# Shared-expert outputs through DRAM as a fifth combine term, three pick buffers and a shorter routing chain in a macaron mixture-of-experts kernel

## The chip, the cores and the metric

One core of one Trainium2 chip runs the whole kernel. The core has five engines that run their own instruction streams and wait for one another by semaphores: TensorE (PE in the profile, its weight loads PEld), VectorE (DVE), ScalarE (ACT), GpSimd (POOL) and SyncE (SP), which here only starts DMAs. The metric is device time in microseconds, the median of several executions; the profile is of one execution.

## The reference

The input x has 4 x 512 tokens of 256 channels, so 2048 tokens. The block is a "macaron": half a feed-forward layer, a scan layer, and the same half feed-forward layer again.

```python
x = L0_attn_x
x = x + 0.5 * _L0_ffn_ref(_layernorm(x), ...)     # gate, shared, 16 routed experts
x = x + _L0_attn_ref(_layernorm(x), ...)          # y_t = a_t * y_(t-1) + x_t, between projections
x = x + 0.5 * _L0_ffn_ref(_layernorm(x), ...)
# in _L0_ffn_ref:
scores = sigmoid(logits) + gate_b
weights, indices = top_k(scores, 4); weights /= weights.sum(-1)
shared_out = (silu(x @ w1_shared) * (x @ w3_shared)) @ w2_shared      # hidden size 176
h3 = silu((x @ w1_routed[e]) * (x @ w3_routed[e]))                    # for the 4 chosen experts e
routed_out = sum over the 4 of weight * (h3 @ w2_routed[e])
return shared_out + routed_out
```

## The kernel before, in words

The tokens lie in 16 tiles of 128 (`NT = 16`). The residual stream stays in SBUF as `xres`. A feed-forward pass `f` (0 or 1) has these stages.

*Norm stage*, 16 tiles. GpSimd normalises a tile (`norm`) into a ring of four buffers, SyncE writes it to `xn_dram` (`xn_out`), TensorE transposes it (`turn_x`), ScalarE copies the high part (`xs_high`), VectorE makes the low part (`xs_low`), and TensorE multiplies by the shared weights and the gate (`hidden`). Products that need float32 accuracy are done as three products of high and low parts (`mm3`). In pass 0 SyncE also loads the routed experts two at a time between the `xn_out`s (`load_experts`, after tiles 1, 4, 7, 10, 13 and 15). Each loaded expert needs a high copy (`high_up`, `high_down`, on ScalarE) and low parts (`low_up` on VectorE for the experts in `DVE_UP`, `low` on GpSimd for the rest). Experts 12 to 15 share their SBUF with the scan layer, so they are loaded and split again in pass 1.

*Routing, shared and pick stage.* VectorE finds the top four of 16 (`route_members`), TensorE counts the members with matmuls (`count`: `p_pre`, L1038, and `p_tot`, L1040), VectorE works out slots (`route_slots`). Meanwhile the shared expert is finished in steps: `shared_step(n)` is, on TensorE, the transpose of hidden tile n (`turn_hidden`, L1012) and the output product of tile n-1 (`shared_out`, L1025), which ends with a matmul by twice the identity that adds `xres` (L1027); on ScalarE, the copy of the transposed tile (`copy_hidden`, L469) and the eviction of tile n-2 with scale 0.5 to `xres` (`evict`, L474). Steps 2 to 9 (`SH_ENDS = 10`) come before the picks, the other seven between them (`picked`). A pick `t` turns the slots of 128 tokens into rows of a token list: VectorE compares (`pick`, L769 and L771), ScalarE scales (`scale_pick`, L487), TensorE multiplies (L1052). The tiles of a pick have two buffers, so that VectorE and ScalarE wait for `s_pkd` of pick t-2. In pass 0 ScalarE's in-order program has one `high_expert` before each of the shared steps 2 to 9, and five more among the picks, expert 15 last; in pass 1 it has experts 12 to 14 ahead of steps 5 to 7 and 15 after pick 13.

*Routed stage*, `NS = 80` slots of 128 rows. GpSimd gathers token rows by indirect DMA (`gather`), four buffers deep; TensorE transposes, multiplies with the slot's expert, transposes the hidden tile, multiplies again; ScalarE and VectorE sit between; SyncE writes the result to `ys_dram` (`y_out`). TensorE enters only after waits for `s_yo` (all shared tiles evicted), `s_rt` (routing ready) and `s_wla`, `s_wlo` (all weight splits done), and the gather of slot 0. On GpSimd the program order is: gathers 0 to 3, then `low_expert(15)`, then gather 4 and the rest.

*Combine.* GpSimd gathers, for each token tile, the rows of the four chosen slots (`combine`, L370, four buffers `cg`); VectorE adds them with their weights to `xres` (L790), two tiles interleaved. In pass 0 the scan layer (L1096 to L1127 on TensorE) runs behind it in chunks of two tiles, in pass 1 SyncE writes the output.

## Time and profile before

| what | value |
|---|---|
| median of 3 runs | 727.38 us (724.78 to 810.8) |
| the profiled execution's own time | 726.9 us |
| its span, first to last instruction | 725.1 us |
| mean granted TensorE clock | 0.868 |
| PE, PEld, DVE, ACT, POOL busy | 73%, 67%, 61%, 47%, 48% of the span |

The span of the profiled execution is 1.8 us shorter than its time. The stages lie, roughly, at: norm stage 7 to 38 us, routing, shared steps and picks 38 to 83, routed stage 92 to 265, combine and scan layer 270 to 384, and then the second pass with its norm stage to 407, routing to 448, routed stage 457 to 631, combine to the end. An engine's busy share is a mean over stages with different limits, so each stage is read by itself.

### The profile page before, as it was taken

The page shows a single profiled execution, that of the slowest core. Times are in us where ns is not written, and L with a number is a line of the kernel's source. Part 1 is how long each engine was busy: PE and PEld are TensorE (multiplying, and loading weights), DVE is VectorE, ACT ScalarE, POOL GpSimd, SP SyncE. Part 2 cuts the span into 40 slices and gives each one's busy share as a digit, 9 for nine tenths or more (in the row PEclk, how much of TensorE's full clock was granted, in tenths as well). Part 3 has the DMA queues.
Part 4 walks back from the last instruction along what each step waited for, and adds up shares of the span by engine and source line. Part 5 has one row for each costly group of instructions (what it writes and reads, how often), then busy time and mean ns, then how long its engine had stood idle before and what let it go on. Part 6 is the DMA issues. An engine that isn't in the chain of part 4 may idle for free.

```text
span 725.1 us, 14307 instructions
## 1 busy us (share of the span) xinstructions
PE 528.3 (73%) x3442; PEld 488.8 (67%) x3443; DVE 440.1 (61%) x1253; ACT 341.3 (47%) x1001; POOL 344.6 (48%) x355
## 2 busy tenths in 40 slices
PE   4887489999999970586667896799999999800000
PEld 3765389999999970365547674699999999700000
DVE  5486547777777753567844686377777777513233
ACT  3568445555555540365564465355555555400000
POOL 2379544444444407777404022544444444067774
PEclk9989879999999995788898989799999999955555
DMA  8950224443434423333202300234343435234443
GB/s 263 298 166 31 66 79 123 126 123 123 123 123 123 122 73 101 102 101 98 64 0 99 108 31 10 81 123 125 121 125 120 128 121 121 80 99 125 130 132 99
DMA packets 51577, 79.92 MB, mean 110 GB/s; under 512 B 8485, under 2 KB 37541, under 8 KB 51549
## 3 DMA queue, kind: packets, MB, share of 16 engines
q0 software_dynamic: 13824, 37.77, 19.3%
q1 hardware_dynamic: 37725, 41.82, 17.6%
q8 instruction: 13, 0.21, 0.1%
q14 instruction: 15, 0.12, 0.1%
HBM read 52.29 MB, written 27.26 MB: 110 GB/s over the span
## 4 chain that ended last, share of the span: by engine, by line
PE 55%; POOL 20%; issue 12%; DMA 4%; ACT 4%; DVE 3%; SPq 0%; POOLq 0%; DVEq 0%; ACTq 0%
PE bank L925 40%; POOL mamba_room L370 17%; PE bank L947 5%; PE bank L981 5%; DMA xn_scratch<-ring_f 3%; POOL ring_f L360 2%; PE bank L1025 2%; ACT ring_f L487 2%; DMA ys_scratch<-ring_f 1%; PE bank L1012 1%; ACT w_routed L406 1%; PE bank L1027 1%; PE bank L990 1%; ACT xres L474 1%; PE bank L1052 1%
## 5 line engine op out<-in xcount | busy, mean ns | idle before, releaser
L925 PE MATMUL bank<-w_routed,ring_r 128*128 (+1 forms) x1920 | 314.7, 313 | 2.8 <-DVE ring_r L647 1.6
L925 PEld LDWEIGHTS bank<-w_routed,ring_r 128*128 128x128 f32 (+1 forms) x1920 | 282.7, 191 | 4.6 <-issue 4.5
L360 POOL DMA_INDIRECT ring_f<-xn_scratch,tokidx x160 | 155.4, 972 | 207.7 <-PE bank L947 176.8
L370 POOL DMA_INDIRECT mamba_room<-ys_scratch,si x128 | 126.6, 989 | 74.5 <-issue 38.4
L790 DVE SCALAR_TENSOR_TENSOR xres<-mamba_room,wk,xres 128x256 f32<-128x256 f32 (+1 forms) x128 | 53.4, 478 | 97.2 <-DMA mamba_room<-ys_scratch,si 97.2
L663 DVE TENSOR_TENSOR ring_f<-bank,ring_f 128x176 f32<-128x176 f32 x160 | 54.5, 341 | 57.7 <-ACT ring_f L441 57.6
L441 ACT ACTIVATE ring_f<-bank 128x176 f32<-128x176 f32 x160 | 50.8, 317 | 81.5 <-PE bank L925 81.5
L655 DVE TENSOR_TENSOR ring_r<-bank,ring_r 88x256 fp32r<-88x256 f32 x160 | 67.3, 421 | 33.3 <-ACT ring_r L433 28.7
L447 ACT ACTIVATE ring_f<-ring_f 128x176 f32<-128x176 f32 x160 | 56.1, 351 | 65.4 <-DVE ring_f L663 65.4
L647 DVE TENSOR_TENSOR ring_r<-bank,ring_r 128x256 fp32r<-128x256 f32 x160 | 66.0, 413 | 17.1 <-ACT ring_r L425 17.1
L673 DVE COPY ring_f<-bank 128x256 f32<-128x256 f32 x160 | 67.8, 424 | 13.2 <-DMA ys_scratch<-ring_f 2.3
L947 PE MATMUL bank<-cst,ring_f 128*128 128x128 f32 x320 | 62.3, 279 | 16.5 <-POOL w_routed L334 16.5
L425 ACT ACTIVATE ring_r<-bank 128x256 fp32r<-128x256 f32 x160 | 59.6, 373 | 17.1 <-PE bank L947 17.1
L981 PE MATMUL bank<-cst,ring_f 128*88 128x128 f32 x320 | 61.5, 273 | 0.0
L433 ACT ACTIVATE ring_r<-bank 88x256 fp32r<-88x256 f32 x160 | 58.0, 362 | 1.1 <-PE bank L981 1.1
L334 POOL TENSOR_TENSOR w_routed<-raw_routed,w_routed 88x512 fp32r<-88x512 f32 (+1 forms) x31 | 44.3, 1456 | 28.9 <-ACT w_routed L409 28.8
L1104 PE MATMUL bank<-mamba_room,stage 128*128 128x256 f32 x128 | 41.4, 480 | 22.4 <-ACT mamba_room L578 21.1
L947 PEld LDWEIGHTS bank<-cst,ring_f 128*128 128x128 f32 x320 | 40.7, 143 | 17.5 <-issue 17.2
L1104 PEld LDWEIGHTS bank<-mamba_room,stage 128*128 128x128 f32 x128 | 30.0, 242 | 31.7 <-ACT mamba_room L578 24.6
L353 POOL TENSOR_SCALAR ring_f<-xres,rstd,nmr 128x256 f32<-128x256 f32 x32 | 18.1, 575 | 61.7 <-DVE nmr L640 41.9
L925 PE MATMUL bank<-w_shared,ring_r 128*128 128x368 f32 x192 | 43.5, 373 | 0.1
L981 PEld LDWEIGHTS bank<-cst,ring_f 128*88 128x88 f32 x320 | 37.1, 123 | 0.2
(118 smaller groups left out, 562.6 us busy)
## 6 DMA issues: line engine op xcount, KB each, us to landing
ys_scratch<-ring_f SPq DMA_DIRECT2D x160, 128.0 KB, 1.7
raw_routed<-in_w13r SPq DMA_DIRECT2D x6, 704.0 KB
xn_scratch<-ring_f SPq DMA_DIRECT2D x32, 128.0 KB, 2.3
raw_routed<-in_w13r SPq DMA_DIRECT2D x8, 352.0 KB
ring_f<-xn_scratch,tokidx POOLq DMA_INDIRECT x160
raw_routed<-in_w2r SPq DMA_DIRECT2D x6, 352.0 KB
xres<-in_x_in SPq DMA_DIRECT2D x4, 512.0 KB, 5.9
mamba_room<-ys_scratch,si POOLq DMA_INDIRECT x128, 2.8
```

Of the source, the lines that this page charges most:

```text
L360: pool.indirect_dma_start(xg[j % UN], None, xn_dram, bass.IndirectOffsetOnAxis(ap=tokidx[:, j:j + 1], axis=0)).then_inc(s_g[j % UN], 16)
L370: pool.indirect_dma_start(cg[t % 4][:, q, :], None, ys_dram, bass.IndirectOffsetOnAxis(ap=si[:, n:n + 1], axis=0)).then_inc(s_cg[t % 4], 16)
L425: act.activation(xT[b][0], p_xT[b][:, 0:DC * P], ACT.Copy).then_inc(s_xhi, 1)
L433: act.activation(hT[b][0][0:HC, :], p_hT[b][0:HC, 0:2 * P], ACT.Copy).then_inc(s_hhi, 1)
L447: act.activation(hid[c % 2], hid[c % 2], ACT.Silu).then_inc(s_s, 1)
L647: dve.tensor_tensor(xT[b][1], p_xT[b][:, 0:DC * P], xT[b][0].bitcast(f32), ALU.subtract).then_inc(s_xlo, 1)
L655: dve.tensor_tensor(hT[b][1][0:HC, :], p_hT[b][0:HC, 0:2 * P], hT[b][0][0:HC, :].bitcast(f32), ALU.subtract).then_inc(s_hlo, 1)
L673: dve.tensor_copy(yb[b], p_y[b][:, 0:D]).then_inc(s_yo, 1)
L925: last = pe.matmul(out, a, b, start=(q == 0), stop=(q == len(terms) - 1))
L947: last = pe.transpose(p_xT[b][:, q * P:(q + 1) * P], xg[k][:, q * P:(q + 1) * P], ident)
L981: last = pe.transpose(p_hT[b][0:HC, q * P:(q + 1) * P], hid[b][:, q * HC:(q + 1) * HC], ident)
L1104: last = pe.matmul(out[:, e * MCH:(e + 1) * MCH], m_w[m][:, q * D + e * P:q * D + (e + 1) * P], src[:, q * MCH:(q + 1) * MCH], start=(q == ...
```

## The change

- `shared_out` on TensorE loses the matmul by `twice`; its eviction goes to one of two new buffers `sh_out` in `ring_f`, and waits for `s_sw` of tile t-2. SyncE writes each to `sh_dram` (16 DMAs of 128 KB per pass) and, after the last `y_out`, reads them back into a fifth place of the combine's buffers (`TERMS = 5`). VectorE adds it by a plain `tensor_tensor`. The next use of a buffer waits for the fifth term.
- Pick tiles have three buffers; VectorE and ScalarE wait for pick t-3.
- VectorE makes the high copies of experts 0 to 3 in pass 0's norm stage (t = 7 to 10) and their low parts at t = 11 to 14. ScalarE's copies there are experts 4 to 6; 7 to 14 lie ahead of shared steps 2 to 6 (two, two, two, one, one), and only expert 15 is left among the picks, after pick 11.
- `DVE_UP` is 0, 1, 2, 3, 15, so GpSimd takes the upper low parts of 13 and 14. `low_expert(15)` comes before the gathers, and before GpSimd's wait for `s_rt`.
- `route_slots`: one product over all four choices in place of four, and no casts back to float; the pick compares with int32 operands. `count` reads `oh` as it lies and writes `p_tot` with a stride.
- SyncE: `twice` isn't loaded; the final output loop is unrolled, with the fifth term's loads in it.

```diff
-DVE_UP = (0, 1, 2, 13, 14, 15)
+NHD = 4
+DVE_UP = (0, 1, 2, 3, 15)
+CHAIN_HIGHS = {2: (7, 8), 3: (9, 10), 4: (11, 12), 5: (13,), 6: (14,)}
+TERMS = TOPK + 1
...
+        sh_out = [ring_f[:, 1536 + b * D:1536 + (b + 1) * D] for b in range(2)]
...
+            def shared_out(f, t):
+                sp.wait_ge(s_yo, f * STEPS + t + 1)
+                sp.dma_start(sh_dram[t * P:(t + 1) * P, :], sh_out[t % 2]).then_inc(s_sw[t % 2], 16)
+
+            def shared_in(f, t):
+                if t >= 4:
+                    sp.wait_ge(s_cd, term(f, t - 4, TERMS - 1))
+                sp.dma_start(cg[t % 4][:, TOPK, :], sh_dram[t * P:(t + 1) * P, :]).then_inc(s_cs[t % 4], 16)
...
                 for e in range(MAMBA_E, NE - 1):
                     load_late(e)
+                for t in range(6):
+                    shared_out(f, t)
                 sp.wait_ge(s_ht, f * STEPS + 8)
                 load_late(NE - 1)
+                for t in range(6, NT):
+                    shared_out(f, t)
...
-                for e in range(0 if f == 0 else MAMBA_E, NE - 1):
-                    low_expert(e, e + 1 + f * (NE - MAMBA_E))
+                for e in range(0 if f == 0 else MAMBA_E, NE):
+                    low_expert(f, e)
                 pool.wait_ge(s_rt, f + 1)
                 for k in range(UN):
                     pool.wait_ge(s_xw[k], 16 * (NT // UN) * (f + 1))
-                for j in range(UN):
-                    gather(f, j)
-                low_expert(NE - 1, NE + f * (NE - MAMBA_E))
-                for j in range(UN, NS):
+                for j in range(NS):
                     gather(f, j)
...
             def evict(f, t):
                 act.wait_ge(s_y, f * STEPS + t + 1)
-                act.activation(xres[:, t, :], p_yS[t % 2][:, 0:D], ACT.Copy, scale=0.5).then_inc(s_yo, 1)
+                if t >= 2:
+                    act.wait_ge(s_sw[t % 2], 16 * (f * (NT // 2) + t // 2))
+                act.activation(sh_out[t % 2], p_yS[t % 2][:, 0:D], ACT.Copy, scale=0.5).then_inc(s_yo, 1)
...
                 for n in range(2, SH_ENDS):
                     if f == 0:
-                        high_expert(f, n + 1)
+                        for e in CHAIN_HIGHS.get(n, ()):
+                            high_expert(f, e)
...
-                    if f == 0 and t % 3 == 1 and t < 12:
-                        high_expert(f, SH_ENDS + 1 + t // 3)
-                    if t == 13:
+                    if t == 11:
                         high_expert(f, NE - 1)
...
-                for k in range(TOPK):
-                    last = dve.tensor_tensor(prod[:, :, k, :], oh[:, :, k, :], sl, ALU.mult)
-                link(last)
+                link(dve.tensor_tensor(prod, oh, sl.unsqueeze(2).broadcast_to((P, NT, TOPK, NE)), ALU.mult))
...
-                dve.tensor_copy(lof, p_loi)
-                link(dve.tensor_copy(hif, p_hii))
...
-                for q in range(TOPK):
+                for q in range(TERMS):
...
+                        if q == TOPK:
+                            dve.wait_ge(s_cs[2 * c + b], 16 * (f * (NT // 4) + i + 1))
...
+                            dve.tensor_tensor(xr, xr, cg[2 * c + b][:, q, :], ALU.add).then_inc(s_cd, 1)
...
-                    if f == 0 and t in (12, 14):
-                        low_up(t // 2 - 6, t // 2 - 5)
+                    if f == 0 and 7 <= t < 7 + NHD:
+                        high_expert(t - 7)
+                    if f == 0 and 7 + NHD <= t < 7 + 2 * NHD:
+                        low_up(f, t - 7 - NHD)
...
+                for b in range(2):
+                    dve.wait_ge(s_sw[b], 16 * (NT // 2) * (f + 1))
                 pipeline(dve, NS, [(LAG_X, dve_x(base)), (LAG_H, dve_product(base)),
...
-                pe.matmul(p_yS[t % 2][:, 0:D], twice, xres[:, t, :], start=False, stop=True).then_inc(s_y, 1)
...
-                    last = pe.matmul(p_tot, hcst[:, H_ONE:H_ONE + P], oh[:, :, k, :].rearrange("p t e -> p e t"),
+                    last = pe.matmul(p_tot.rearrange("p (e t) -> p t e", e=NE), hcst[:, H_ONE:H_ONE + P], oh[:, :, k, :],
```

## Rows read from the trace of the kernel before

**Rows 1.** The page's chain that ended last, by line, in shares of the span.

```profile
PE bank L925 40%; POOL mamba_room L370 17%; PE bank L947 5%; PE bank L981 5%; DMA xn_scratch<-ring_f 3%; POOL ring_f L360 2%; PE bank L1025 2%; ACT ring_f L487 2%; DMA ys_scratch<-ring_f 1%; PE bank L1012 1%; ACT w_routed L406 1%; PE bank L1027 1%; PE bank L990 1%; ACT xres L474 1%; PE bank L1052 1%
```

**Rows 2.** Busy time by stretch, then granted TensorE clock, DMA share and GB/s.

```profile
45.00:50.00 5.00, 5.00 (x17) 3.06 (x15) 3.01 (x10) 2.25 (x5) 3.44 (x3) 0.54 0.43 131
...
430.00:440.00 10.00, 7.79 (x65) 5.86 (x66) 9.30 (x19) 6.04 (x15) 0.00 (x0) 1.00 0.00 0
```

**Rows 3.** The chain in order of time, end of pass 0's picks: start, length.

```profile
79.82 0.68 ACT w_routed L406
...
81.02 0.91 ACT ring_f L487 x2
...
82.71 0.16 DVE tokidx L778
...
83.14 3.13 POOL ring_f L360
```

**Rows 4.** The same chain at the end of pass 1's picks.

```profile
446.09 0.91 ACT ring_f L487 x2
...
448.20 3.00 POOL ring_f L360
```

**Rows 5.** ScalarE's timeline: start, length, what.

```profile
26.26 0.80 ACT L406 ACTIVATE w_routed<-raw_routed 128x704 fp32r<-128x704 f32 x1
...
60.42 1.04 ACT L487 ACTIVATE ring_f<-ring_f,cst 128x320 f16<-128x320 f16 x2
...
428.91 1.00 ACT L487 ACTIVATE ring_f<-ring_f,cst 128x320 f16<-128x320 f16 x2
```

**Rows 6.** TensorE's timeline, its idle time and who ended it in brackets.

```profile
45.19 1.88 PE L1040 MATMUL bank<-ring_f,hcst 128*128 128x256 f16 x4
...
52.77 1.03 PE L1025 MATMUL bank<-raw_shared 88*128 88x256 f32 x4
53.64 0.60 PE L1027 MATMUL bank<-xres,stage 128*128 128x256 f32 x2
...
92.14 1.09 PE L947 MATMUL bank<-cst,ring_f 128*128 128x128 f32 x4 [8.40 <-POOL w_routed L334]
...
456.89 1.09 PE L947 MATMUL bank<-cst,ring_f 128*128 128x128 f32 x4 [8.07 <-POOL w_routed L334]
```

**Rows 7.** VectorE's timeline in pass 0.

```profile
26.14 0.42 DVE L678 TENSOR_TENSOR ring_r<-bank,ring_r 128x256 fp32r<-128x256 f32 x1 [3.78 <-ACT ring_r L454]
...
31.68 0.88 DVE L689 TENSOR_TENSOR w_routed<-raw_routed,w_routed 128x704 fp32r<-128x704 f32 x1
...
51.79 1.42 DVE L755 TENSOR_TENSOR ring_f<-ring_f,bank 128x256 f32<-128x256 f16 x4
...
55.30 0.23 DVE L762 CAST bank<-bank 128x64 f32<-128x64 int32 x1
...
55.70 0.49 DVE L769 TENSOR_TENSOR ring_f<-hcst,bank 128x320 f16<-128x320 f16 x1
56.10 0.68 DVE L771 TENSOR_TENSOR ring_f<-hcst,bank 128x512 f16<-128x512 f16 x1
...
61.50 0.49 DVE L769 TENSOR_TENSOR ring_f<-hcst,bank 128x320 f16<-128x320 f16 x1 [3.72 <-PE bank L1052]
```

**Rows 8.** GpSimd's timeline in pass 0.

```profile
29.03 1.63 POOL L353 TENSOR_SCALAR ring_f<-xres,rstd,nmr 128x256 f32<-128x256 f32 x3 [3.02 <-DMA xn_scratch<-ring_f]
...
34.24 5.05 POOL L334 TENSOR_TENSOR w_routed<-raw_routed,w_routed 88x512 fp32r<-88x512 f32 x3
...
49.46 24.32 POOL L334 TENSOR_TENSOR w_routed<-raw_routed,w_routed 88x512 fp32r<-88x512 f32 x17 [1.08 <-ACT w_routed L409]
```

**Rows 9.** DMA issues of the page: KB each, median us from issue to landing.

```profile
ys_scratch<-ring_f SPq DMA_DIRECT2D x160, 128.0 KB, 1.7
...
mamba_room<-ys_scratch,si POOLq DMA_INDIRECT x128, 2.8
```

**Rows 10.** VectorE's last combine, at the end of pass 1.

```profile
719.71 2.86 DVE L790 SCALAR_TENSOR_TENSOR xres<-mamba_room,wk,xres 128x256 f32 x7 [4.12 <-DMA mamba_room<-ys_scratch,si]
```

More of the change, by code:

```diff
@@ L180, in build @@
         s_wsd = sem("shared_down_loaded")
+        s_cs = [sem(f"shared_fetched{b}") for b in range(4)]
+        s_sw = [sem(f"shared_written{b}") for b in range(2)]
         s_hs = sem("shared_hidden_turned")
@@ L320, in _ @@
                         y_out(f, i, k)
+                for b in range(2):
+                    sp.wait_ge(s_sw[b], 16 * (NT // 2) * (f + 1))
+                for t in range(NT if f == 0 else 4):
+                    shared_in(f, t)
             o_v = out_d.rearrange("(t p) d -> p t d", p=P)
-            with sp.Fori(0, NT // 2) as i:
-                for b in range(2):
-                    t = i * 2 + b
-                    sp.wait_ge(s_cd, NT * TOPK + i * 2 * TOPK + 2 * (TOPK - 1) + b + 1)
-                    sp.dma_start(o_v[:, ds(t, 1), :], xres[:, ds(t, 1), :]).then_inc(s_out, 16)
+            for t in range(NT):
+                sp.wait_ge(s_cd, term(1, t, TERMS - 1))
+                sp.dma_start(o_v[:, t:t + 1, :], xres[:, t:t + 1, :]).then_inc(s_out, 16)
+                if t + 4 < NT:
+                    shared_in(1, t + 4)
             sp.wait_ge(s_out, 16 * NT)
```

92 lines of the change are left out of this document (53 added, 39 removed).

## The prediction, as it was put on record

> **What bounds the kernel now.** I read the page's chain by line first: 40% of the span is TensorE's routed products (L925) and 17% GpSimd's combine gathers (L370) [rows 1]. The change touches neither, so those two stages are fixed, and the question is how long it takes to get from the norm stage to the routed stage. Next I followed the chain in order of time. In pass 0 it runs through ScalarE at the end of the picks, then the token list is ready at 82.87 (82.71 + 0.16), GpSimd issues the first gather at 83.14, which takes 3.13 [rows 3], and TensorE starts at 92.14, released not by a gather but by GpSimd's low part of expert 15, after 8.40 idle [rows 6]. Pass 1 looks the same: last scaled pick at 447.00 (446.09 + 0.91), first gather at 448.20 taking 3.00 [rows 4], TensorE at 456.89, again released by L334 [rows 6]. So the stretch has four parts that end one another: ScalarE's way to the first pick, the picks, the first gather, and expert 15. In the combine the chain stays on GpSimd, and VectorE waits for gathers [rows 10]; more work there shows only behind the last gather.
>
> **Order on GpSimd, the start of the routed stage.** Expert 15's low part now comes before `s_rt`, so TensorE should wait for gather 0 instead. An indirect DMA of the combine lands 2.8 after the start of its issue, the issue taking 0.95, so 1.85 after the issue's end [rows 9, 10]. From the token list: 0.3 to the issue, 3.13 (3.00 in pass 1), 1.85 and some 0.15 to the transpose, 5.4 (5.3) in all. Before it was 92.14 - 82.87 = 9.3 in pass 0, and 456.89 - 447.94 = 8.95 in pass 1 (the list was ready 0.94 after the last scaled pick in both). Gain 3.9 and 3.6. The condition is that expert 15 is ready in time. In pass 0 GpSimd starts its low parts at 34.24 [rows 8]. It has four lower parts of the experts that VectorE copied, at 1.3 to 1.7 each (5.05 for three) [rows 8], eleven pairs (4 to 14), and the part of expert 15. A pair costs (24.32 - 1.28)/8 = 2.88, since the x17 of rows 8 is eight pairs and one lower part. The sum is 34.2 + 6 + 31.7 + 1.3 = 73 to 74. ScalarE copies expert 15 after pick 11, at about 70 by the times below. With the list ready at 75.6, this is hidden by 1 to 3; if it isn't, the excess goes one for one onto the path. In pass 1 GpSimd has only four experts and is idle long before.
>
> **Getting to the first scaled pick, pass 0.** Before, at 60.42 [rows 5]. Up to about 53, TensorE at the low clock sets the pace (granted 0.54 of full in 45 to 50, its engine busy all the time [rows 2]) and ScalarE has gaps; from there ScalarE is back to back, with one expert (0.68 + 0.52 = 1.20, from 79.82 to 81.02 [rows 3]) and about 0.53 for copy and eviction per step. The new order puts eight experts ahead of steps 2 to 6 in place of 2 to 9. Step by step: two experts each fit into the first gaps; ScalarE is then full until its copy of step 6 at about 53.8; steps 7 to 9 have 0.53 of its work each. What is late next? TensorE needs 0.87 (52.77 to 53.64 [rows 6]) and a transpose of 0.22, 1.1 a step, now that the residual matmul is gone (0.43 at full clock, since the 0.60 of L1027 contains a pipelined 0.2; so 0.85 at half). And the eviction waits for the write of two tiles earlier: 0.37 + 1.9 (landing 1.7 [rows 9] and 0.2 of semaphores), 2.3 for two tiles. So 1.1 to 1.2 a step, and the last of these evictions ends at about 57.1. VectorE is no limit: `p_tot` cost 4 x 0.43 [rows 6] and may cost half (0.85 less), the one product costs at most what the four do (1.42; I count no gain), and the two casts with their wait are 0.4 (55.30 to 55.70 [rows 7]); its first pick starts at 55.7 - 1.25 = 54.4, and with three buffers it has three ready by then. Gain 3.3.
>
> **A loss in the norm stage, pass 0.** VectorE copies 704 and 512 columns four times. The trace has no such copy on VectorE; bounds are 0.6 (half of ScalarE's 1.2) and 1.5 (as the two-input L689, 0.88 for 704 [rows 7]). VectorE is idle 3.78 before tile 9 [rows 7] and some 0.5 before most others, so the copies fit; the four low parts at t = 11 to 14 (before: two) leave it at most 1 behind, just when TensorE still has three `hidden`s queued. ScalarE now copies expert 4 at tile 9, where it copied 0 at 26.26 [rows 5]. Experts 4 and 5 are loaded after tile 7's write, and tile 8's write, queued behind that load, landed only at 29.03 [rows 8], so the load itself at about 28.5. ScalarE may stand still until then, with the transposed tiles 10 and on behind it, some 1.2 late, and it catches up little before tile 15. The price is 0 to 1.5; I take 0.8. The first scaled pick is then at 57.9.
>
> **The picks.** Pass 0 took 81.93 - 60.42 = 21.5. That is ScalarE's in-order program, with a round trip to TensorE in each of the seven shared steps; VectorE's waits are for it, as the 3.72 of rows 7. Four experts fewer are 4.8 less: 16.7, to 74.6, list at 75.6. VectorE gives a pick each 1.0 (55.70 to 56.70 [rows 7]) against 16.7/16 = 1.05, so the third buffer is needed here and just suffices. Gain at the list 82.87 - 75.6 = 7.3. Pass 1: before, 428.91 to 447.00, 18.1, with two waits of 0.6 for VectorE, which three buffers remove: 17. Its first scaled pick was TensorE-bound; the removed matmuls (0.85 twice, then 0.43 a step) and `p_tot` would bring more than 4, but ScalarE's experts 12 to 14 at steps 5 to 7 and the write waits of the last evictions hold it at about 427.2, 1.7 earlier. Gain 1.7 + 1.0 = 2.7.
>
> **The fifth term.** One more operation per tile, two behind the last gather of each pass, 0.41 apart like the seven in 2.86 [rows 10]: 0.8 at the end, and 0.8 in pass 0 before the scan layer's tail. Elsewhere it hides in VectorE's waits of 4 a pair (4.12 in rows 10); those are also what GpSimd's wait for the fifth term has in hand. SyncE's 16 writes and 16 reads a pass of 128 KB land long before use; queued behind its waits are only expert 15's load (needed 14 later), the scan weights, and in pass 1 the outputs. Writes still in flight delay VectorE's entry into the routed stage until about 78.5, TensorE's start being later: nothing. Not loading `twice` is nothing.
>
> **Sum.** Pass 0: 7.3 + 3.9 = 11.2, less 0.5 because the scan weights' load (768 KB) shares the DMA engines with gather 0. Pass 1: 2.7 + 3.6 = 6.3. Off 17.0, on 1.6: 15.4. From the profiled execution's 726.9, which is 0.5 below the median 727.38, that gives 711.5. With the bounds of the norm stage, of the write waits (1.7 to 2.3 of landing for six steps a pass) and of the GpSimd sum, this case alone spans 706 to 717.
>
> **A rule against it.** Before, `p_tot` reads its member matrix with a stride and takes 0.43 a matmul at half clock; after, the stride is on the PSUM side, and no row shows a strided write. Bounds: free (0.21 each), or as slow as now, 0.43. As slow as now, it puts 0.85 on TensorE's queue in each pass, ahead of `turn_hidden(3)`, so 1.7 in all: 713. I take free, since the slow case of rows 6 is a strided read. The Trainium skill (SBUF — State Buffer, Door 1: The DMA port swizzle) states that "any non-contiguous PSUM access pattern significantly slows down matmuls", which speaks for that second value; no row here bears it out so far.
>
> **Rivals.** *The stride costs as before*: 713. *Late supply*: GpSimd's splits of pass 0 end at 76 to 78 rather than 74, or the evictions wait 2.5 and more for their writes. For it: splits wait on a port when VectorE works too (5.05 for three against 3.8). Against: the mean of 17 already holds that. 2 to 3 in pass 0, up to 2 each for the writes: 717 to 720. *The clock falls*: TensorE has less to do in shared steps and picks. At half clock the picks' round trips cost 0.35 each, seven a pass, and the shared steps 1.0 more for some six steps: 8 a pass at most, 16 in all, so 720 to 727. Against it: at 7.79 busy of 10 the clock stays at 1.00 [rows 2], and the busy share hardly falls as the stage shortens with it. *Slower than before*: the pick compares now read int32. If such a compare ran at half speed, VectorE would give a pick per 2.0, 32 a pass in place of 17: 711.5 + 2 x 15 = 741. From 1.53 a pick it eats the whole gain. Against it: L762 reads 64 int32 in 0.23 like its float neighbours [rows 7]. *More than forecast*: no loss in the norm stage, and pass 1's first pick earlier by the whole 4: 706 or less.
>
> **How the numbers follow.** Forecast 0.50, stride 0.17, late supply 0.15, clock 0.07, slower 0.04, more 0.07. The range from 704 to 720 leaves out the slower case, most of the clock case and the far ends of the others, some 2 in 10. A change of 2% (14.5, so 712.8) is about what a measurement of this kernel can tell from none. It lies just above the likeliest value: six in ten of the forecast case, four in ten of the stride case and the last case give faster by over 2%, 0.45; within 2% 0.51; slower 0.04.
>
> **What would show it.** After: TensorE's L947 at the start of each routed stage released by a gather, 5.4 after the token list; ScalarE's L487 starting near 57.9 and 427.2; picks of 16.7 and 17; L1040 at 0.21 a matmul at half clock; POOL L334 done before `tokidx`; two more operations behind the last gather. It is wrong if VectorE waits for nothing in the picks, if L454 shows a long wait at tiles 9 to 14, or if the granted clock in the picks is under 0.9.

## The result, and the profile after

The changed kernel took 715.33 us (median of 4 runs, 713.42 to 716.63), the kernel before beside it 727.18. The ratio is 0.985, with an interval from 0.981 to 0.989: about 11 us or 1.5% faster. The forecast was 711.5 with a range from 704 to 720, and put 0.51 on "within 2%". One of the four executions of the kernel before took 810.8, in a slower state of the chip, and the ratio and its interval leave it out. The profiled execution took 713.42 with a span of 711.6 (before 726.9 and 725.1), which is 13.5 less, against a sum of 15.4 forecast.

The stage table shows where these 13.5 went. Each time is a start in the timelines (us from the span's start), pass 0 and pass 1.

| | before | after | stage grew by | forecast |
|---|---|---|---|---|
| sigmoid of the logits | 38.03 / 407.61 | 41.16 / 402.73 | +3.1 / 0.0 | +0.8 / 0 |
| first scaled pick | 60.42 / 428.91 | 61.26 / 421.78 | -2.3 / -2.25 | -3.3 / -1.7 |
| token list ready | 82.86 / 447.93 | 79.40 / 440.16 | -4.3 / -0.6 | -4.8 / -1.0 |
| ScalarE's first copy of a transposed x | 92.88 / 457.64 | 84.05 / 444.56 | -5.4 / -5.3 | -3.9 / -3.6 |
| first copy of a `hidden` | 96.03 / 460.78 | 88.75 / 447.80 | +1.55 / +0.1 | +0.5 / 0 |
| first combine gather | 270.70 / 636.06 | 263.27 / 622.26 | -0.15 / -0.8 | 0 / 0 |
| pass 1 starts / the end | 384.03 / 725.1 | 379.19 / 711.6 | +2.6 / +0.3 | +0.8 / +0.8 |

The sigmoid of pass 1 is counted from the start of that pass. The sum is -13.5: the total was met by errors of both signs. Pass 0 gained 4.8 where 9.9 were forecast, pass 1 8.7 where 5.5 were.

Views of the profile after show the places. First the page's chain by line, which answers to [rows 1].

```profile
PE bank L965 41%; POOL mamba_room L399 12%; PE bank L987 5%; PE bank L1021 5%; DMA mamba_room<-ys_scratch,si 4%; DMA xn_scratch<-ring_f 3%; DVE xres L824 2%; DMA ring_f<-xn_scratch,tokidx 1%; DMA ys_scratch<-ring_f 1%; ACT ring_f L515 1%; POOL ring_f L382 1%; DVE xres L827 1%; PE bank L1065 1%; PE bank L1030 1%; PE bank L1092 1%
```

The routed products (L965) stand as before. The combine gathers (L399) hold 12% where L370 held 17%, and VectorE's combine lines (L824, L827) and the landing of gathers have come in beside them, a first hint that the fifth term may not be free. L360, GpSimd's first gather before, is gone from the list.

The chain in order of time at the end of pass 0's picks, and TensorE's timeline where both routed stages start, answer to [rows 3, 4, 6].

```profile
75.81 0.42 PE bank L1092 x4
76.23 0.43 PE bank L1052 x2
76.67 1.71 PE bank L1065 x4
78.38 0.55 PE bank L1092 x8
...
79.25 0.16 DVE tokidx L809
79.41 0.28 issue
79.69 1.52 POOL ring_f L389
81.21 0.31 issue
81.52 4.71 DMA ring_f<-xn_scratch,tokidx
```

```profile
48.71 1.91 PE L1080 MATMUL bank<-ring_f,hcst 128*128 128x256 f16 x4
...
83.27 0.69 PE L987 MATMUL bank<-cst,ring_f 128*128 128x128 f32 x2 [2.51 <-DMA ring_f<-xn_scratch,tokidx]
86.27 0.69 PE L987 MATMUL bank<-cst,ring_f 128*128 128x128 f32 x2 [2.31 <-DMA ring_f<-xn_scratch,tokidx]
...
443.79 0.69 PE L987 MATMUL bank<-cst,ring_f 128*128 128x128 f32 x2 [2.95 <-DMA ring_f<-xn_scratch,tokidx]
```

L1080 is `p_tot` with its strided write: 1.91 for four, as the strided read took before [rows 6]. TensorE is released by a gather now, 3.9 and 3.6 after the list instead of 9.3 and 8.95. The first gather took 1.52 (1.40 in pass 1) instead of 3.13 (3.00), which the forecast hadn't taken off. Slot 1 of pass 0 comes late: its gather is 4.71 on the way, and TensorE is idle 2.31 a second time.

ScalarE's timeline answers to [rows 5].

```profile
30.24 0.79 ACT L432 ACTIVATE w_routed<-raw_routed 128x704 fp32r<-128x704 f32 x1 [3.19 <-DMA raw_routed<-in_w2r]
...
61.26 1.00 ACT L515 ACTIVATE ring_f<-ring_f,cst 128x320 f16<-128x320 f16 x2
...
421.78 1.00 ACT L515 ACTIVATE ring_f<-ring_f,cst 128x320 f16<-128x320 f16 x2
```

The copy of expert 4 waits 3.19 for its weights, the stall that the forecast named, later (30.24 instead of 28.5) and longer than it said.

In the combine of pass 0 GpSimd's and VectorE's timelines are to be read side by side. First a gather of the kernel before and the statistics over it, then the changed kernel's.

```profile
284.64 1.28 POOL L370 DMA_INDIRECT mamba_room<-ys_scratch,si  x1 [0.30 <-issue]
285.13 0.75 DVE L627 BATCH_NORM_STATS2 lg<-xres 128x6 f32<-128x256 f32 x2
```

```profile
328.73 0.95 POOL L399 DMA_INDIRECT mamba_room<-ys_scratch,si  x1 [0.30 <-issue]
329.99 1.09 POOL L399 DMA_INDIRECT mamba_room<-ys_scratch,si  x1 [0.30 <-issue]
331.38 1.95 POOL L399 DMA_INDIRECT mamba_room<-ys_scratch,si  x1 [0.30 <-issue]
333.63 0.95 POOL L399 DMA_INDIRECT mamba_room<-ys_scratch,si  x1 [0.30 <-issue]
```

```profile
328.98 2.86 DVE L824 SCALAR_TENSOR_TENSOR xres<-mamba_room,wk,xres 128x256 f32<-128x256 f32 x7 [2.22 <-DMA mamba_room<-ys_scratch,si]
331.75 0.76 DVE L827 TENSOR_TENSOR xres<-xres,mamba_room 128x256 f32<-128x256 f32 x2
332.54 0.75 DVE L654 BATCH_NORM_STATS2 lg<-xres 128x6 f32<-128x256 f32 x2
```

A gather is 0.95 as a rule. The one that lies under the statistics of VectorE takes 1.95 and ends with them (333.33, they at 333.29). Four of the 64 in this pass do that and none before. There the gathers end with the statistics too, but these begin 0.49 after a gather and not 1.16, so that it takes 1.28. In pass 1, whose combine has no statistics, the largest is 1.25.

The windows of the picks answer to [rows 2]; their columns are the busy time of each engine, the granted clock, and the DMA share and rate.

```profile
60.00:70.00 10.00, 7.67 (x64) 5.14 (x62) 9.28 (x20) 7.38 (x20) 10.00 (x8) 1.00 0.37 122
70.00:80.00 10.00, 7.71 (x49) 5.84 (x50) 6.66 (x15) 6.23 (x15) 6.35 (x6) 0.74 0.15 52
...
430.00:440.00 10.00, 7.39 (x55) 5.46 (x56) 6.65 (x15) 6.94 (x17) 1.26 (x1) 0.83 0.15 53
```

The clock was at full over both stretches before; now it falls to the lower level (1.2 GHz) in the last 4 of each pass's picks, where the chain above has four L1065 in 1.71. In both passes TensorE has just been idle for 1.61, while ScalarE copied expert 15. From the first scaled pick to the list the granted clock is 0.87 and 0.91.

### The profile page after: what moved, and what is told of

It is laid out like the page before. It is cut to its first block, busy times and chain, and to the rows that moved or that the text cites. A ratio compares the mean times of both kernels' runs of the same rounds, so it can differ in the third digit from the quotient of the medians.

```text
span 711.6 us, 14277 instructions
## 1 busy us (share of the span) xinstructions
PE 516.8 (73%) x3378; PEld 477.4 (67%) x3379; DVE 449.6 (63%) x1280; ACT 336.8 (47%) x993; POOL 349.2 (49%) x358
## 4 chain that ended last, share of the span: by engine, by line
PE 54%; POOL 13%; issue 11%; DMA 10%; DVE 8%; ACT 3%; DVEq 1%; SPq 0%; POOLq 0%; ACTq 0%
PE bank L965 41%; POOL mamba_room L399 12%; PE bank L987 5%; PE bank L1021 5%; DMA mamba_room<-ys_scratch,si 4%; DMA xn_scratch<-ring_f 3%; DVE xres L824 2%; DMA ring_f<-xn_scratch,tokidx 1%; DMA ys_scratch<-ring_f 1%; ACT ring_f L515 1%; POOL ring_f L382 1%; DVE xres L827 1%; PE bank L1065 1%; PE bank L1030 1%; PE bank L1092 1%
## 5 line engine op out<-in xcount | busy, mean ns | idle before, releaser
L965 PE MATMUL bank<-w_routed,ring_r 128*128 (+1 forms) x1920 | 314.6, 313 | 0.6 <-DVE ring_r L674 0.3
L965 PEld LDWEIGHTS bank<-w_routed,ring_r 128*128 128x128 f32 (+1 forms) x1920 | 282.6, 191 | 2.2 <-issue 2.1
L389 POOL DMA_INDIRECT ring_f<-xn_scratch,tokidx x160 | 152.2, 951 | 185.4 <-PE bank L987 173.8
L399 POOL DMA_INDIRECT mamba_room<-ys_scratch,si x128 | 128.4, 1003 | 73.3 <-issue 35.6
L824 DVE SCALAR_TENSOR_TENSOR xres<-mamba_room,wk,xres 128x256 f32<-128x256 f32 (+1 forms) x128 | 53.4, 479 | 89.4 <-DMA mamba_room<-ys_scratch,si 89.4
L360 POOL TENSOR_TENSOR w_routed<-raw_routed,w_routed 88x512 fp32r<-88x512 f32 (+1 forms) x34 | 48.6, 1458 | 31.8 <-ACT w_routed L435 31.8
L382 POOL TENSOR_SCALAR ring_f<-xres,rstd,nmr 128x256 f32<-128x256 f32 x32 | 19.9, 628 | 63.7 <-DVE nmr L667 43.0
L965 PE MATMUL bank<-w_shared,ring_r 128*128 128x368 f32 x192 | 43.7, 374 | 1.2 <-DVE ring_r L705 1.2
```

Source lines behind the costliest of these rows:

```text
L389: pool.indirect_dma_start(xg[j % UN], None, xn_dram, bass.IndirectOffsetOnAxis(ap=tokidx[:, j:j + 1], axis=0)).then_inc(s_g[j % UN], 16)
L399: pool.indirect_dma_start(cg[t % 4][:, q, :], None, ys_dram, bass.IndirectOffsetOnAxis(ap=si[:, n:n + 1], axis=0)).then_inc(s_cg[t % 4], 16)
L824: dve.scalar_tensor_tensor(xr, cg[2 * c + b][:, q, :], wk[:, ds(t * TOPK + q, 1)], xr, ALU.mult, ALU.add).then_inc(s_cd, 1)
L965: last = pe.matmul(out, a, b, start=(q == 0), stop=(q == len(terms) - 1))
```

## The experiments

All ratios below are to the kernel before on the same chip. They ran in three groups of four, each on its own chip, where the kernel before took 726.5, 753.4 and 727.6. On the second, ScalarE stands still in the scan stage of every kernel, which takes 14 to 23 longer there, and the last combine takes 6 to 9 longer; so I use its kernels by stage, and their totals only by ratio.

**The norm stage's wait for expert 4.** (`norm_no_load_wait`) ScalarE's copies of experts 4 and 5 are taken two tiles later.

```
-CHAIN_HIGHS = {2: (7, 8), 3: (9, 10), 4: (11, 12), 5: (13,), 6: (14,)}
+CHAIN_HIGHS = {2: (6, 7), 3: (8, 9), 4: (10, 11), 5: (12,), 6: (13,), 7: (14,)}
...
-                    if f == 0 and 9 <= t < 15:
+                    if f == 0 and 11 <= t < 15:
...
```

> The changed kernel, with ScalarE's copy of expert 4 at tiles 11 and 12 in place of 9 and 10, expert 5 at 13 and 14, and experts 6 to 14 ahead of shared steps 2 to 7 (two, two, two, one, one, one). Theory A: the 3.1 us that the sigmoid of pass 0 comes later (41.16 against 38.03) is mostly ScalarE's stand of 3.19 us for the load of experts 4 and 5; then the sigmoid comes at about 39.5 and the first scaled pick 1 to 1.5 us earlier than 61.26, the total 1 us less. Rival B: the loads themselves arrived later in that execution and the queue of writes behind them sets the pace; then the sigmoid stays at 40.5 to 41.5 whatever ScalarE does, and the total does not move.

Result: 714.42, ratio 0.984 (0.980 to 0.988), beside 0.985 of the changed kernel: not told apart. The wait is gone: L432 follows L484 without idle time.

```profile
29.02 0.32 ACT L484 ACTIVATE raw_routed<-bank 128x176 f32<-128x176 f32 x1
29.22 0.80 ACT L432 ACTIVATE w_routed<-raw_routed 128x704 fp32r<-128x704 f32 x1
```

The sigmoid came at 39.07 instead of 41.16 and the first scaled pick at 59.88 instead of 61.26, both as theory A had them; the total didn't follow. From the sigmoid to the first scaled pick it took 20.8 instead of 20.1, and the combine and scan stage of pass 0, which this edit doesn't touch, took 119.8 instead of 115.9. And the eleven other profiled executions with the changed kernel's norm stage have their sigmoid anywhere from 39.07 to 42.50 (median 40.53), and the two with the norm stage of before at 38.03 and 38.30. So the change costs this stage 1 to 4.5. How much of that is the order of ScalarE's copies, and how much the moment at which the loads land, one execution of this edit doesn't part.

**The scan weights' load.** (`scan_weights_late`) SyncE waits for the third transposed x before it issues the 768 KB.

```
                     sp.wait_ge(s_yo, NT)
+                    sp.wait_ge(s_xt, NT + 3)
```

> The changed kernel, with the load of the scan weights (768 KB) started only after TensorE has transposed slot 2 of pass 0's routed stage. Theory A: the gather of slot 1, which landed 4.71 us after the start of its issue and let TensorE's second transposes wait until 86.27, was held up by that load on the DMA engines; without it slot 1 is ready 1.3 us after slot 0, as in pass 1 (443.79 and 444.84), and the total is 1.5 us less. Rival B: the gathers of the first slots land late by themselves in pass 0; then nothing moves. In both the SyncE writes of the first slots start a little later and cost nothing.

Result: 714.35, ratio 0.982 (0.977 to 0.987). TensorE's first two transposes:

```profile
82.31 0.69 PE L988 MATMUL bank<-cst,ring_f 128*128 128x128 f32 x2 [2.53 <-DMA ring_f<-xn_scratch,tokidx]
83.46 0.69 PE L988 MATMUL bank<-cst,ring_f 128*128 128x128 f32 x2 [0.45 <-DMA ring_f<-xn_scratch,tokidx]
```

The second wait is 0.45 instead of 2.31. From the first copy of a transposed x to the first `hidden` 3.24 went by instead of 4.70 (4.5 to 5.0 in the other executions that start this stage alike): 1.5 on the path, where the forecast had taken 0.5. The total isn't told apart from the changed kernel's 0.985.

**Why the first gather is short.** (`dve_up_three`) VectorE has its low parts of three experts behind the token list again, as before.

```
-DVE_UP = (0, 1, 2, 3, 15)
+DVE_UP = (0, 1, 2, 3, 13, 14, 15)
```

> The changed kernel, with the upper low parts of experts 13 and 14 back on VectorE (three tensor_tensors of 0.88 us after the token list, as before, in place of one). Theory A: the first gather of a routed stage is held while VectorE runs them; it took 3.13 and 3.00 us with three and 1.52 and 1.40 with one, so it is back at 3.0 to 3.1 here, and TensorE starts 1.6 us later in each pass. Rival B: the first gather's length comes from what GpSimd ran before it (code or another operation), which stays as changed here; then it stays at 1.4 to 1.5.

Result: 715.77 (one run, so that the total says little). The gather is 3.13 (3.01 in pass 1) again.

```profile
77.53 3.13 POOL L389 DMA_INDIRECT ring_f<-xn_scratch,tokidx  x1 [3.50 <-DVE tokidx L809]
80.96 0.95 POOL L389 DMA_INDIRECT ring_f<-xn_scratch,tokidx  x1 [0.30 <-issue]
```

```profile
76.86 0.23 DVE L808 TENSOR_SCALAR te<-bank 1x80 int32<-1x80 f32 x1 [2.15 <-PE bank L1092]
77.02 0.22 DVE L809 CAST tokidx<-bank 128x80 int32<-128x80 f32 x1
77.17 2.47 DVE L726 TENSOR_TENSOR w_routed<-raw_routed,w_routed 128x704 fp32r<-128x704 f32 x3
```

VectorE's three subtractions end at 79.64 and the gather 1.0 later at 80.66. With one subtraction (0.87) they end at 80.19 and the gather at 81.21, 1.0 later too. The gather makes little way beside these subtractions, which read two tensors from SBUF. Its records are rough, but the distance to the next gather's start says the same: 3.43 against 1.83. TensorE's first transpose came 2.4 and 2.95 later after the list than in the changed kernel, more than the 1.6 expected: from the end of the gather's issue to that transpose 2.9 and 3.3 went by instead of 2.1 and 1.95, and no run says why. In pass 0 the later start meets no second wait, so that the first `hidden` is only 0.95 later there. The Trainium skill (GPSIMD Engine Reference, Key points) states that GpSimd contends with VectorE instructions "with two SBUF inputs"; this trace agrees, with 1.6 on one gather. Beside the combine's scalar_tensor_tensors, which read two tensors of SBUF as well, little of it shows: gathers there take 0.95 to 1.28.

**The statistics under a gather: is it the kind of instruction?** (`fifth_stt`) The fifth term is written as a scalar_tensor_tensor, like the other four.

```
-                            dve.tensor_tensor(xr, xr, cg[...][:, q, :], ALU.add)...
+                            dve.scalar_tensor_tensor(xr, cg[...][:, q, :], 1.0, xr, ALU.mult, ALU.add)...
```

> The changed kernel, with the fifth term added by scalar_tensor_tensor (times 1.0, plus) in place of tensor_tensor; same operands, same result. In pass 0 four of the combine's 64 gathers last 1.95 us, each beside the two tensor_tensors of L827 and nothing like it in the trace of before, where the worst beside scalar_tensor_tensors and statistics last 1.28. Theory A: GpSimd's descriptor writing stands while VectorE runs a tensor_tensor with two SBUF inputs, and does not for a scalar_tensor_tensor; then no gather lasts over 1.35 and pass 0's 64 gathers sum to 64.3 us in place of 66.2, the total 1.5 to 2 us less. Rival B: it is the fifth term's loads from DRAM that share the queues or the DMA engines with the gathers; then the 1.95s stay.

Result: 714.9, ratio 0.983 (0.979 to 0.987). Gathers at 1.95 stay, six of them: the kind of the fifth instruction isn't the cause. The other executions whose combine is the changed kernel's have 4 to 7 on the first and the last chip. Again each ends with the statistics (318.97 + 1.95 = 320.92, they at 320.88).

**No trip through DRAM.** (`no_dram`) The rest of the change stays, and the shared outputs go the way of before.

```
-                act.activation(sh_out[t % 2], ...)
+                act.activation(xres[:, t, :], ...)
...
+                pe.matmul(p_yS[t % 2][:, 0:D], twice, xres[:, t, :], start=False, stop=True).then_inc(s_y, 1)
```

> The changed kernel without its DRAM path: the matmul by twice the identity is back, the eviction goes to xres with no wait for a write, and the combine has four terms; everything else as changed. Theory A: the path is worth little in all: it frees TensorE in the shared steps (first scaled pick some 1 us earlier in pass 0, 2 to 3 in pass 1, where TensorE sets the pace) and costs 2.6 us in pass 0's combine and scan stage (115.92 against 113.33) and 0.3 to 0.8 behind the last gather; so this kernel is within 1.5 us of the changed one, either way. Rival B: the path is what brought the gain of 12 us, and this kernel stands at 722 to 727.

Result: 735.85, ratio 0.975 (0.971 to 0.979), against 0.985 of the changed kernel on another chip. Neither theory had it so: it isn't within 1.5 of the changed kernel, nor slower, but faster. No gather is at 1.95; the longest is 1.67; the statistics begin 0.89 after its start, and it ends with them. `before_pool_order`, which hasn't the fifth term either, has one such gather as well. The total called for both kernels on one chip (last group, below).

**GpSimd's order alone** (`before_pool_order`), in the kernel before: expert 15's low part ahead of the first gathers, nothing else.

```
-                for e in range(0 if f == 0 else MAMBA_E, NE - 1):
+                for e in range(0 if f == 0 else MAMBA_E, NE):
...
-                for j in range(UN):
-                    gather(f, j)
-                low_expert(NE - 1, NE + f * (NE - MAMBA_E))
```

> The kernel before with one edit: GpSimd's low part of expert 15 ahead of its wait for the routing, and so ahead of the first gathers, in both passes. Theory A: this alone lets TensorE start with gather 0: 3.9 us earlier in pass 0 (less up to 1.5 for the scan weights' load, which meets the first gathers) and 3.6 in pass 1, total 5.5 to 7.5 us less, half of the whole change's gain. Rival B: in pass 0 ScalarE copies expert 15 so late (after pick 13, at 81.0) that GpSimd's part, 1.3 us, ends only at the token list, and in both passes TensorE's next wait takes the place of the one removed; gain under 3 us.

Result: 748.96, ratio 0.993 (0.991 to 0.996), some 5 us. TensorE is released by gathers in both passes.

```profile
90.45 1.12 PE L944 MATMUL bank<-cst,ring_f 128*128 128x128 f32 x4 [6.49 <-DMA ring_f<-xn_scratch,tokidx]
```

From the list to the first copy it takes 8.15 and 5.92, where 10.0 and 9.71 were needed before: 1.9 and 3.8. Pass 1 gives the forecast 3.6; pass 0 gives half, and all four transposes start together. I read that as the gathers held back by the scan weights' load; no run takes the load away from this kernel, but the last group does so for one that has the same wait. In the changed kernel this part gives 5.4 and 5.3. In pass 1 the short first gather is the rest; in pass 0 it is 1.6 of 3.5.

**Two pick buffers.** (`picks_two`)

```
-                if t >= 3:
-                    dve.wait_ge(s_pkd, f * NT + t - 2)
+                if t >= 2:
+                    dve.wait_ge(s_pkd, f * NT + t - 1)
...
-                dve.tensor_tensor(pickB[t % 3], ...
+                dve.tensor_tensor(pickB[t % 2], ...
...
```

ScalarE's wait and the other two buffers, `pickA` and `pickS`, are changed alike.

> The changed kernel with two pick buffers in place of three (waits for pick t-2). Theory A: with ScalarE's experts gone from the picks, VectorE's one pick per 1.0 us is near ScalarE's 1.05, and two buffers cost about 1 us in pass 0 and 0.7 to 1 in pass 1: total 1.5 to 2.5 more. Rival B: the third buffer buys nothing, since ScalarE's round trips to TensorE set the pace; the picks take 16.9 and 17.1 from first to last as now.

Result: 743.34, ratio 0.985 (0.981 to 0.989). First scaled pick to list is 19.80 and 20.40, against 18.14 and 18.38 with three: the third buffer is worth 1.7 and 2.0. ScalarE's timeline has two waits for VectorE, like those that the prediction named for pass 1 before:

```profile
64.18 0.56 ACT L515 ACTIVATE ring_f<-ring_f,cst 128x320 f16<-128x320 f16 x1 [0.56 <-DVE ring_f L800]
...
72.08 0.56 ACT L515 ACTIVATE ring_f<-ring_f,cst 128x320 f16<-128x320 f16 x1 [0.56 <-DVE ring_f L800]
```

They are 1.1 in all; the granted clock over the picks is 0.81 and 0.73, against 0.87 and 0.91 with three buffers. The clock isn't tied to the buffers alone, though: `scan_weights_late`, which has three, shows 0.88 and 0.75.

**The strided `p_tot`, by itself.** (`count_three`) Before the real four matmuls, two more sets of four write the same bank and are overwritten: one contiguous on both sides (L1080), one that reads its members with a stride, as before (L1082). L1084 is the changed kernel's, which writes with a stride.

```
+                    pe.matmul(p_tot, hcst[:, H_ONE:H_ONE + P], oh[:, :, k, :], ...)
...
+                    pe.matmul(p_tot, hcst[:, H_ONE:H_ONE + P], oh[:, :, k, :].rearrange("p t e -> p e t"), ...)
```

> The changed kernel with eight matmuls more in the count of each pass, ahead of those of p_tot and overwritten by them: four with the member matrix read as it lies and the sums written side by side, then four with the strided read of before; the last four, as changed, read as it lies and write with a stride. Same operands, same size, same clock if it holds. Theory A: a strided PSUM write is as slow as the strided read: 0.21 us, 0.43, 0.43 a matmul at half clock. Rival B: all three cost the same, 0.43, and the stride is no cause: then p_tot's matmuls were slow for another reason. Rival C: the write is cheap and the 0.43 of the changed kernel was the clock alone. The total is 1.2 to 2.5 us a pass more, which is not the point.

Result: 747.63 (one run; eight matmuls more in each pass).

```profile
48.09 1.06 PE L1080 MATMUL bank<-ring_f,hcst 128*128 128x256 f16 x4
48.95 1.91 PE L1082 MATMUL bank<-ring_f,hcst 128*128 128x256 f16 x4
50.68 1.89 PE L1084 MATMUL bank<-ring_f,hcst 128*128 128x256 f16 x4
```

Less the pipelined part of 0.2, a matmul is 0.21 contiguous, 0.43 with a strided read and 0.42 with a strided write, all at half clock; pass 1 has 1.06, 1.91 and 1.89 as well. The eight matmuls more are 2.6, and from the sigmoid to the first scaled pick pass 0 takes 22.67 where seven executions of kernels with the same stage take 20.10 to 20.12: TensorE's time at this place lies wholly on the path. The Trainium skill's sentence on non-contiguous PSUM access (SBUF — State Buffer, Door 1: The DMA port swizzle) is borne out: a factor of two here.

**The last group: four kernels on one chip.** The changed kernel once more (`changed_again`):

> The changed kernel once more, unchanged, on the chip of the next three kernels, so that they can be set against it. Ratio to the kernel before as measured first, 0.985 (0.981 to 0.989). Some four of pass 0's combine gathers at 1.95 us, each ending where VectorE's two bn_stats end, and none in pass 1.

Result: 716.72 (714.13 to 719.3), ratio 0.986 (0.982 to 0.989). Without the trip through DRAM, as above (`no_dram_again`):

> The changed kernel with the shared outputs' way of before: ScalarE writes 0.5 of the shared output with the residual, which TensorE adds through the product with 2I, straight into xres; no trip through DRAM, no fifth term. Theory A (the trip costs more than it gives back: the routed tokens' pass 0 combine meets the statistics at the wrong moment, 2 to 5 us, and pass 1 has a term more behind its last gathers): ratio to the changed kernel beside it 0.987 to 0.993, no gather at 1.95 us in pass 0, the first scaled pick 0.5 to 1.5 us later after the sigmoid than in the changed kernel. Theory B (the 1 per cent between the two earlier calls is the chips'): ratio to the changed kernel 0.998 to 1.003.

Result: 708.67 (706.55 to 710.96), ratio 0.973 (0.970 to 0.976). That is 0.987 of the changed kernel beside it (0.973 / 0.9855), 8 us less: the way through DRAM loses, the difference wasn't the chips'. The two profiled executions are the changed kernel's fastest run (714.13) and this one's slowest (710.96), so that they show only 3.1 of it: from the first combine gather to pass 1 118.1 against 114.0, from pass 1's first gather to the end 89.3 against 88.2, and on the other side sigmoid to first scaled pick of pass 1 20.0 against 21.2. So in these two executions the trip saves 2.0 on the way to the first picks (0.8 and 1.2; the second is less sure, since this stretch of pass 1 runs from 18.8 to 21.1 over the executions with the trip and from 18.3 to 21.2 without) and loses 5.2 in the combines and 0.9 in the picks (below); the rest of the 8 isn't placed. Of the 4.1 in pass 0's combine, 2.0 lie between the first gather and the last, which follow one another 0.30 apart in both, and 2.0 behind the last (32.4 against 30.4). The windows of the picks (same columns as above):

```profile
62.00:79.00 17.00, 14.59 (x117) 10.69 (x117) 13.56 (x29) 12.10 (x30) 12.70 (x9) 1.00 0.01 2
422.00:438.00 16.00, 13.59 (x110) 9.88 (x111) 13.22 (x26) 11.74 (x30) 2.64 (x2) 1.00 0.00 1
```

With the residual product back in, TensorE is busy 14.6 of 17 and its clock is full; in the changed kernel it is 12.7 of 17 over the same stretch with 0.88 granted. First scaled pick to list is 17.6 in both passes, against 18.1 and 18.0, although there is more to multiply. All the profiles agree in this: the five kernels with the residual product have the clock at 1.00 in their ten stretches of picks, and the nine without it from 0.73 to 0.95 in their eighteen. But every kernel with the product is also one without the writes to DRAM, so that no run parts the two.

Without the trip TensorE's first transpose in pass 0 starts 5.5 after the list, against 3.5 in pass 1: here the scan weights' load seems to meet gather 0, as the forecast had it, and costs 2.0; the last version below bears that out.

Then the changed kernel with the shared term added first (`fifth_first`):

```
                         if q == 0:
-                            dve.wait_ge(s_cg[2 * c + b], ...)
+                            dve.wait_ge(s_cs[2 * c + b], ...)
...
-                        if q == TOPK:
-                            dve.wait_ge(s_cs[2 * c + b], ...)
+                        if q == 1:
+                            dve.wait_ge(s_cg[2 * c + b], ...)
...
-                        if q < TOPK:
+                        if q > 0:
-                            dve.scalar_tensor_tensor(xr, cg[2 * c + b][:, q, :], wk[:, ds(t * TOPK + q, 1)], xr, ...)
+                            dve.scalar_tensor_tensor(xr, cg[2 * c + b][:, q - 1, :], wk[:, ds(t * TOPK + q - 1, 1)], xr, ...)
...
```

> The changed kernel with the shared term added first instead of last: VectorE waits for the load of the shared rows, adds them, and only then waits for the gathers. Nothing is left out. Theory A (the fifth term costs by where it stands: behind the last gather of a tile it pushes the statistics onto the following gather): no gather at 1.95 us in pass 0, first combine gather to start of pass 1 2 to 4 us shorter than in the changed kernel, pass 1 ends 0.7 us nearer to its last gather, total 2 to 5 us less. Theory B (the gathers are long by where they stand against any work of VectorE's): as many gathers at 1.95 us, pass 0 as in the changed kernel, and only the 0.7 us of pass 1.

Result: 710.09 (708.95 to 712.88), ratio 0.976 (0.973 to 0.979), 0.990 of the changed kernel: 6.6 less by the medians, 3.9 by the spans. Over the statistics that follow on a pair, the gathers are these:

```profile
273.85 1.19 POOL L399 DMA_INDIRECT mamba_room<-ys_scratch,si  x1 [0.30 <-issue]
275.34 1.28 POOL L399 DMA_INDIRECT mamba_room<-ys_scratch,si  x1 [0.31 <-issue]
```

```profile
272.94 2.86 DVE L824 SCALAR_TENSOR_TENSOR xres<-mamba_room,wk,xres 128x256 f32<-128x256 f32 x7 [4.52 <-DMA mamba_room<-ys_scratch,si]
275.84 0.75 DVE L654 BATCH_NORM_STATS2 lg<-xres 128x6 f32<-128x256 f32 x2
```

None is at 1.95. The statistics follow on the last term again, and begin 0.50 after the gather (0.49 in the kernel before) instead of 1.16; the gather ends with them either way (276.62, they at 276.59), so that it is 1.28 and not 1.95. That a gather isn't through after 1.16 can be read as well: under a chain of terms alone, as in pass 1, the longest gather takes 1.2 to 1.3 in every one of these kernels. From the first combine gather to pass 1 it takes 114.6 instead of 118.1: most of what the trip costs is where its term stands. Of these 3.5, 1.2 lie in the gathers and 2.3 behind the last one (30.1 against 32.4), a stretch that runs from 30.5 to 32.8 in the executions with the term last; how much of it the order of the terms brings, they don't say. Pass 1's combine gained 0.2 of the 0.7 expected.

Last, the version to which the runs point: no trip through DRAM, the scan weights late, and VectorE's low part of expert 15 ahead of the token list, in its wait for the last pick products (`no_dram_early_low`).

```
...
                 for t in range(NT):
                     pick(f, t)
-                route_end(f)
                 for e in DVE_UP:
                     if e >= MAMBA_E:
                         low_up(f, e)
+                route_end(f)
...
```

> The changed kernel without the trip through DRAM, with the scan weights' load put behind TensorE's third routed transpose, and VectorE's low part of expert 15 taken before the token list (in the 2.1 us in which it waits for the last pick products) instead of after it. Nothing is left out. If the first gather is long by VectorE's subtraction beside it, it takes 0.9 to 1.1 us here (1.5 and 1.4 in the changed kernel), and TensorE's first routed transpose comes 0.4 us earlier after the list in each pass; slot 1 of pass 0 gains 1.5. Sum: 2 to 2.5 us below the kernel without the trip alone. If the gather has that length anyway: 1.5 us below it, all in pass 0.

Result: 705.2 (701.87 to 709.2), ratio 0.968 (0.965 to 0.972): 3.2% faster than before, 1.7% faster than the changed kernel (0.9683 / 0.9855).

```profile
80.53 1.14 POOL L382 DMA_INDIRECT ring_f<-xn_scratch,tokidx  x1 [3.05 <-DVE tokidx L800]
...
435.30 0.99 POOL L382 DMA_INDIRECT ring_f<-xn_scratch,tokidx  x1 [3.03 <-DVE tokidx L800]
```

The first gather is 1.14 and 0.99, and the subtraction lies in a wait of VectorE's that was 2.11 long. From the list to the first `hidden` it takes 7.0 and 6.8, against 9.4 and 7.2 without these two edits, 2.4 and 0.4 less. The 0.4 is the short gather, in both passes, and the 2.0 that pass 0 has above it are those of its late first transpose, which now starts 3.2 after the list and not 5.5: this part is the load's. Together 2.8 where 2 to 2.5 were expected; the medians differ by 3.5.

## Why the prediction held, step by step

The range held the time and the verdict was the likelier one, but by 13.5 = 4.8 + 8.7 where the sum had 9.9 + 5.5. That the sum came so near is luck: terms missed by up to 3 and cancelled. One of the signs that the prediction gave for being wrong came about as well: the granted clock in the picks of pass 0 is 0.87, under 0.9. A long wait at tile 9 came too, though ahead of the expert's copy (L432) and not of the transposed x. Point by point:

- **Order on GpSimd, the start of the routed stage.** The mechanism was right (gathers release TensorE, `before_pool_order` gives 3.8 in pass 1). The size was off by one term, the first gather's 3.13: I took its length in [rows 3] as its own. VectorE's three subtractions lay beside it (2.47 from 82.78 in its timeline, which I hadn't read that far); the change leaves one. Forecast 3.9 and 3.6, measured 5.4 and 5.3. Expert 15 was ready in time: GpSimd was idle 3.58 before the first gather.
- **The scan weights' load** was put at 0.5 against gather 0. It hit gather 1, and took 1.5. In the kernels without the trip it did meet gather 0, and took 2.0 (`no_dram_again` against `no_dram_early_low`).
- **A loss in the norm stage.** The place was right, the size wasn't: 3.1 in this execution, 1 to 4.5 over the eleven, 2.4 by their median, against 0 to 1.5. The bound held only the load's landing at 28.5, and the copy started at 30.24.
- **Getting to the first scaled pick.** From the sigmoid on it gained 2.3 against 3.3, and 0.85 of the missing 1.0 is the strided `p_tot`: here I took the lower bound, "free", and it was the upper. `count_three` shows both the price and that it lies on the path. Pass 1 gained 2.25 against 1.7 in the profiled execution. Seven others with the same stage take 18.8 to 21.1 here (20.0 in the middle), where before took 21.3, so that the usual gain is 1.3 and this one was luck.
- **The picks** took 18.1 to the list against 17.7 in pass 0 and 18.4 against 18.0 in pass 1. The third buffer was needed, and worth 1.7 and 2.0 rather than 1. "The clock falls" was a rival at 0.07, and I said against it that the busy share hardly falls. It did fall, in the last 4 of each pass. The change takes a matmul of 0.43 out of every shared step, and what speaks for this as the cause is that all ten stretches of picks with that matmul are at full clock and none of the eighteen without it; `no_dram_again` takes 0.5 and 0.4 less in them. It isn't shown alone: no run changed the busy share and nothing else.
- **The fifth term** is the step that failed. It was put at 0.8 in each pass, all of it behind the last gather, and "elsewhere it hides in VectorE's waits". It does hide there, in VectorE's time; in GpSimd's it doesn't: two more operations of VectorE's (0.76) let the statistics begin 0.67 later over a gather, which ends with them. Measured, 2.6 in pass 0 (4.1 to the kernel without it, on one chip), 0.3 in pass 1 (1.1). The 2.6 is the mildest of the five profiles that have this combine and aren't from the second chip: the others have 3.7 to 6.5, with 4 to 7 long gathers. Their gathers, put at nothing, account for 2.0 to 4.9 of it, and what lies behind the last gather for 0.5 to 2.5, where 0.8 was forecast. `fifth_first` shows that the place of the term makes the gathers long, `fifth_stt` that its kind doesn't.
- **Rivals.** *The stride costs as before* was true. *Late supply* of GpSimd's splits wasn't: they took 38.75 where the sum had 39, and ended at 76.1 since they began 3 late, like the list. *Slower*, by int32 compares, wasn't: L800 takes 0.48 as L769 did.

## What to carry to other kernels

An operation that is hidden in one engine's waits still moves what follows it, and that can land on another engine that shares something with it. Before calling it free, look at what stands behind it and beside whom it will run; where the order of a sum is free, put the term whose data come early first.

A length read in one surrounding isn't the operation's own: a gather took 0.95, 1.5, 1.95 and 3.1 here, by what VectorE did beside it. And when a change takes work off an engine whose granted clock can fall, see what the clock says before counting the saving.

## What the runs showed of the hardware

- An indirect gather's issue on GpSimd is 0.95 with VectorE idle, and 0.95 to 1.28 beside the combine's chain of scalar_tensor_tensor and tensor_tensor of 128x256. Beside VectorE's tensor_tensor of 128x704 with two inputs in SBUF it ends 1.0 after the last of them (1.52 with one, 3.13 with three). Why the long ones hold it and the short ones hardly do, no run settles.
- Two bn_stats of 128x256 (0.75) that begin while the issue runs hold it up, and it ends with them: it takes 1.28, 1.67, 1.95 and 2.35 when they begin 0.49, 0.89, 1.16 and 1.56 after it, with or without a fifth term. Two gathers, in `after` and `before_pool_order`, are exceptions: with statistics 0.7 and 0.8 after them they take 1.15 and 1.21 and end before them.
- A matmul of 256 fp16 columns that writes PSUM with a stride takes twice a contiguous one (0.42 against 0.21 at half clock), just as one with a strided read.
- A granted clock of 0.73 to 0.95 over the picks goes with the kernels that lack a small product (0.43) in each shared step, and 1.00 with those that have it, in all twenty-eight stretches. The writes to DRAM differ between them too.
- 768 KB of loads issued behind the first gathers made one of them late, by 1.5 to 2.0 on the path.
